# A two-layer decoder kernel: products of constants ahead of the second stage's attention, its loads issued in two parts, and the fifth stage's keys and values prepared in the third stage and kept in DRAM

## The chip, the cores and the metric

The kernel runs on one core of one Trainium2 chip. The metric is the device time of one execution in microseconds (us); lower is better. All times here are of the kernel before the change.

## What is computed

A decoder of two layers works on x of 2048 tokens (32 sequences of 64) by 256 features, all in float32. Six sub-layers follow each other, each x = x + f(layernorm(x)):

```python
x = x + attention_L0(ln(x))        # 16 heads of 128, with biases
x = x + cross_L0(ln(x), ctx, ctx)  # 32 query heads of 8, 8 key heads, no mask
x = x + ffn_L0(ln(x))              # gated, 1024 wide, gate modulated by a small attention
x = x + memory_L1(ln(x))           # cumulative sums of cos and sin features
x = x + cross_L1(ln(x), ctx, ctx)  # 16 heads of 16, rms norm of q and k, rope, causal
x = x + ffn_L1(ln(x))              # gated, 2048 wide, 4-bit weights
```

For this change two lines of the reference matter. The second sub-layer is a plain softmax attention over 64 context rows. In the fifth, keys and values come from the context alone, so they can be computed at any time:

```python
q, k = rms_norm(q, q_norm_w), rms_norm(k, k_norm_w)      # k, v: ctx, the same for all of x
q, k = q * cos + rotate_half(q) * sin, k * cos + rotate_half(k) * sin
```

## The kernel before, in words

**Tiles.** x stays in SBUF as 16 tiles (`NT`) of 128 tokens by 256 features, two sequences to a tile. Each of five stages opens with a block `token_stats` (mean and variance of every token, a square root on ACT, a reciprocal on DVE) and ends in a barrier of all engines. The fifth Python stage holds the last two sub-layers; this text calls the sub-layers "stages" one to six, as the tile names do (s2, s3a, s3f, s5a, s6f).

**Order.** Nothing schedules the work: each engine has its own program, written with `run_steps` (L87). It gets parts with a lag each; at step s the part of lag l works on unit s - l. Engines meet at counted semaphores (`wait_ge`, `then_inc`).

**Stage two** (`stage_L0_cross`, L611 to 825) has 32 units, two (r = 0 and 1) for each tile. For one unit PE does `scores` (8 products of 32x64 by 256 columns, L786), `turn(0)` and `turn(1)` (4 transposes of 128x128 each, L798), `weigh(0)` and `weigh(1)` (8 products each, L814), and once per tile `turn_x` (2 transposes, L774). DVE takes the maximum (L714) and subtracts it (L718); both read the one scores buffer, and `scores` of the next unit waits for `shifted`. ACT does the exponential (L740) and copies the turned weights out of PSUM (L746). POOL normalises x (L678) and spreads the keys (L682). PE's order within a step is scores, weigh(0), turn(0), weigh(1), turn(1), turn_x. All 8 loads of the context are issued by SP inside the `token_stats` block, two for each chunk of 4 tiles (L631, L633).

**Stage three's feed-forward** (`feed_forward`, L1190) has 32 units (4 groups of 4 tiles by 8 slices). A unit is 13 products of 512 columns (L1244, L1253) and 12 of 256 (L1264), all in the fp32r type. DVE multiplies (L1293), ACT copies the high part (L1282), POOL subtracts the low part (L1316), and `down` of the unit comes two steps later.

**Stage five** (`stage_L1_cross`, L1968) issues 5 loads beside `token_stats`, then has a block s5k in which DVE squares, norms and ropes the keys (L2018 to 2057) and POOL spreads the values (L2065, L2071), and then `attention16` (L838) in mode "L1". PE's order there is scores, turn(0), final, turn_qk, turn(1), weigh(0), turn_att, weigh(1). The 32 loads of stage six's weights are issued by SP beside it (L2191).

**Stage six** is `token_stats` with 16 BATCH_NORM_STATS (L213), then `split_tokens` and `feed_forward`.

Of the kernel before, what the change touches and what calls it, by code (L numbers as in the profile page):

```python
# [16 lines left out]
P = 128  # L17
# [106 lines left out]
class Core:  # L124


    def __init__(self, nc, ctx, ins):
# [5 lines left out]
        self.stats_ready = False  # L133
        self.stored_weights = nc.dram_tensor("stored_weights", (PIECES, P, 6 * D), F32, kind="Internal").ap()
# [475 lines left out]
def stage_L0_cross(core):  # L610
# [7 lines left out]
    with ExitStack() as octx:  # L618
# [9 lines left out]
        def load_context(sp):  # L628
            for n in range(NT // CHUNK):
# [11 lines left out]
        with ExitStack() as ctx:  # L641
# [122 lines left out]
            def _(pe):  # L764
                pe.wait_ge(zeroed, 1)

                def turn_x(u, rnd, n):
# [55 lines left out]
                run_steps(pe, U, [(scores, 3), (weigh(0), 5), (turn(0), 4), (weigh(1), 5), (turn(1), 4),  # L823
# [10 lines left out]
def attention16(core, mode, tag, mv, rstd, factor, w, zT=None, mT=None, beside=None, prefetch=None):  # L834
# [6 lines left out]
    with ExitStack() as ctx:  # L841
# [58 lines left out]
        def _(dve):  # L900
            nc.vector.tensor_copy(ident_r[:, :], core.c("ident")).then_inc(masks, 1)
            nc.vector.tensor_copy(mask_r[:, :], core.c("mask_add")).then_inc(masks, 1)
            if own:
                dve.wait_ge(zeroed, 2)

# [41 lines left out]
            steps(dve, [(attended, 4), (shift, 2)] + ([(spread_values, 1)] if own else []) + [(finish, 5)])  # L947

        @block.gpsimd
        def _(pool):  # L950
# [29 lines left out]

            steps(pool, [(residual if own else rope, 0)])
# [4 lines left out]
        def _(act):  # L986
# [56 lines left out]

            if own:
# [7 lines left out]
        def _(pe):  # L1052
            pe.wait_ge(masks, 2)

# [135 lines left out]
def feed_forward(core, tag, zT, gate_w, up_w, down_w, F, kind, mod=None, ready=None, stats=False):  # L1190
# [11 lines left out]
    with ExitStack() as ctx:  # L1202
# [10 lines left out]
        block = ctx.enter_context(nc.Block())  # L1213

# [58 lines left out]
        def _(act):  # L1273
# [5 lines left out]
            def high(u, rnd, f):  # L1279
# [4 lines left out]
            run_steps(act, U, split_modulation(True, act) + [(activate, 0), (high, 0)],  # L1284
                      unroll=FC)

        @block.vector
        def _(dve):
# [7 lines left out]
            def add(u, rnd, f):  # L1296
# [11 lines left out]
            run_steps(dve, U, split_modulation(False, dve) + [(multiply, 0), (add, 2)],  # L1308
                      unroll=FC)

        @block.gpsimd
        def _(pool):
# [6 lines left out]
            run_steps(pool, U, [(low, 0)], unroll=FC)  # L1319

def stage_L0_ffn(core):
    nc, ins = core.nc, core.ins
    F, R = 1024, 16
    with ExitStack() as ctx:
# [17 lines left out]
        w["in"] = room.sb("in", [P, NC, F])  # L1346
        w["up"] = room.sb("up", [P, NC, F])
        w["down"] = room.sb("down", [P, F // P, D])
# [122 lines left out]
        def part_of(name):  # L1471
# [5 lines left out]
                     stats=True)  # L1477
# [490 lines left out]
def stage_L1_cross(core, prefetch):  # L1968
    nc, ins = core.nc, core.ins
    H, KV, E = 16, 4, 16  # L1970
    W = KV * E
    with ExitStack() as ctx:
# [5 lines left out]
        q_cos = room.sb("q_cos", [P, D])  # L1978
        q_sin = room.sb("q_sin", [P, D])
# [3 lines left out]
        with ExitStack() as sctx:  # L1983
            sroom = Room(nc, sctx, "s5k")
            raw = sroom.sb("raw", [P, NT, W])
            values = sroom.sb("values", [P, NT, 2, W])
            qw = sroom.sb("qw", [P, D])
            kn = sroom.sb("kn", [P, NT, W])
            rot = sroom.sb("rot", [P, NT, W])
            kw = sroom.sb("kw", [P, W])  # L1990
            ss = sroom.sb("ss", [P, NT])
            root = sroom.sb("root", [P, NT])
            inv = sroom.sb("inv", [P, NT])
            loaded, step_done, rooted, summed, v_done = sroom.sems("loaded", "step_done", "rooted", "summed", "v_done")

            def load_context(sp):
                sp.dma_start(raw[:, :, :].rearrange("p t d -> p (t d)"), ins["ctx_rows"]).then_inc(loaded, 16)
                sp.dma_start(kw[:, :], ins["L1_xattn_k_norm_w"].rearrange("(a n) -> a n", a=1).to_broadcast([P, W])) \
                    .then_inc(loaded, 16)
                sp.dma_start(qw[:, :], ins["L1_xattn_q_norm_w"].rearrange("(a n) -> a n", a=1).to_broadcast([P, D])) \  # L2000
                    .then_inc(loaded, 16)
                sp.dma_start(wo[:, :, :], ins["L1_woT"].rearrange("(c p) n -> p c n", p=P)).then_inc(loaded, 16)
                sp.dma_start(values[:, :, :, :].rearrange("p t b d -> p (t b d)"), ins["ctx_values"]).then_inc(loaded, 16)
# [341 lines left out]
```

## Time and profile before

| what | value |
|---|---|
| median of 3 runs | 1947.82 us (1945.99 to 1949.38) |
| the profiled execution's own time | 1944.22 us |
| its span | 1942.4 us |
| mean granted TensorE clock | 0.902 of full speed |
| PE busy | 1711.3 us (88%) |
| DVE busy | 1134.2 us (58%) |
| ACT busy | 842.3 us (43%) |
| POOL busy | 686.1 us (35%) |

The span runs from the first to the last instruction; the time of the execution is 1.8 us longer. Busy PE time counts matmuls from start to modelled end, so a high share doesn't say at what clock the engine ran. The clock stands apart: it is granted at full speed (1.00, 2.4 GHz) or at half (0.50, 1.2 GHz). The stages, by the trace: one to 568 us, two to 761, three to 1086 (its feed-forward from 948), four to 1508, five to 1639, six to the end.

### The profile page before, as it was taken

To read this page: it belongs to the slowest core of one execution; us is meant where nothing else is said; L and a number is where in the kernel's file an instruction comes from. 1 tells how busy PE (TensorE), PEld (TensorE's weight loads), DVE (VectorE), ACT (ScalarE), POOL (GpSimd) and SP (SyncE) were. 2 spreads that over 40 slices of the span, in tenths; PEclk is the share of its full clock that TensorE was granted. 3 is DMA by queue.
4 is the path that set the end of the run, shared out by engine and by line. 5 is a ranking of instruction groups with operands and counts; after the bars stand their busy time and mean duration, and the time that the engine had idled before them with its cause. 6 is when DMAs were issued, how large, how long until landed. Compare 5 with 4: busy or idle time off the path is not lost. (4 is left out here: it accounts for less than half of the span.)

```text
span 1942.4 us, 33715 instructions
## 1 busy us (share of the span) xinstructions
PE 1711.3 (88%) x12986; PEld 1324.9 (68%) x12986; DVE 1134.2 (58%) x1820; ACT 842.3 (43%) x1399; POOL 686.1 (35%) x508
## 2 busy tenths in 40 slices
PE   4999999999959996889999786899998297999997
PEld 3888888888846665668788562444444275788886
DVE  6676767676765555565322495999897666211111
ACT  3555555555533433444422325555562275322222
POOL 0111221122123431640122204999996341223232
PEclk9999999999975555789999896999999598899999
DMA  3011111111120002000000000000000440000001
GB/s 94 15 58 55 63 38 57 54 62 38 57 98 2 1 2 92 2 2 2 2 1 1 19 18 0 1 1 1 0 1 0 157 146 2 1 1 1 1 0 43
DMA packets 49490, 57.56 MB, mean 30 GB/s; under 512 B 7216, under 2 KB 43568, under 8 KB 49248
## 3 DMA queue, kind: packets, MB, share of 16 engines
q1 hardware_dynamic: 49376, 55.97, 8.9%
q8 instruction: 80, 1.31, 0.3%
q14 instruction: 34, 0.28, 0.0%
HBM read 41.28 MB, written 14.68 MB: 29 GB/s over the span
## 5 line engine op out<-in xcount | busy, mean ns | idle before, releaser
L543 POOL TENSOR_TENSOR s_w_parts<-s_w_raw,s_w_parts 128x768 fp32r<-128x768 f32 x16 | 29.7, 1854 | 428.8 <-ACT s_w_parts L495 428.8
L1293 DVE TENSOR_TENSOR s6f_hid<-s6f_act_sb,s6f_u_ps 128x512 f32<-128x512 f32 x64 | 44.0, 687 | 219.5 <-PE s6f_u_ps L1244 219.5
L1316 POOL TENSOR_TENSOR s6f_hid_parts<-s6f_hid,s6f_hid_parts 128x512 fp32r<-128x512 f32 x64 | 82.7, 1293 | 230.5 <-ACT s6f_hid_parts L1282 230.5
L1826 POOL TENSOR_TENSOR s4b_pcs<-s4b_cs,s_p_rows 128x1024 f32<-128x1024 f32 x64 | 120.8, 1913 | 95.4 <-ACT s4b_cs L1872 95.4
L1837 POOL TENSOR_TENSOR s4b_with_re<-s4b_with_re,s4b_with_im 128x1024 f32<-128x1024 f32 x64 | 150.9, 2385 | 2.6 <-DVE s4b_with_im L1791 2.6
L1912 PE MATMUL s4b_c_ps<-s4b_pcs,const 128*128 128x512 f32 x256 | 122.3, 600 | 0.0
L419 PE MATMUL s_v_ps<-s_wv_parts,s_xnT 128*128 128x256 f32 x768 | 103.8, 285 | 12.0 <-ACT s_v L524 6.4
L478 PE MATMUL s_o_ps<-s_w_parts,s_zT 128*128 128x256 f32 x768 | 110.2, 294 | 4.1 <-DVE x_rows L582 4.1
L419 PEld LDWEIGHTS s_v_ps<-s_wv_parts,s_xnT 128*128 128x128 f32 x768 | 96.3, 191 | 17.6 <-ACT s_v L524 9.7
L1902 PE MATMUL s4b_turns_ps<-s_theta_bd,s_zc 128*128 128x512 f32 x128 | 78.1, 694 | 31.4 <-DVE s4b_frac L1776 30.4
L1316 POOL TENSOR_TENSOR s3f_hid_parts<-s3f_hid,s3f_hid_parts 128x512 fp32r<-128x512 f32 x32 | 41.3, 1291 | 180.2 <-ACT s3f_hid_parts L1282 180.2
L1264 PEld LDWEIGHTS s6f_o_ps<-s6w_parts,s6f_hid_parts 128*128 128x128 f32 x768 | 99.1, 188 | 6.6 <-issue 1.0
L1282 ACT ACTIVATE s6f_hid_parts<-s6f_hid 128x512 fp32r<-128x512 f32 x64 | 40.5, 632 | 145.1 <-PE s6f_o_ps L1264 140.9
L478 PEld LDWEIGHTS s_o_ps<-s_w_parts,s_zT 128*128 128x128 f32 x768 | 97.0, 192 | 8.8 <-issue 4.5
L1244 PE MATMUL s6f_g_ps<-s_zT,s6w_parts 128*128 128x512 f32 (+1 forms) x384 | 101.8, 401 | 1.2 <-PEq L257 1.2
L437 PE MATMUL s_q_ps<-s_xnT,s_w_parts 128*128 128x512 f32 x384 | 102.5, 403 | 0.0
L1264 PE MATMUL s6f_o_ps<-s6w_parts,s6f_hid_parts 128*128 128x256 f32 x768 | 100.5, 279 | 0.8 <-POOL s6f_hid_parts L1316 0.8
L1244 PE MATMUL s6f_u_ps<-s_zT,s6w_parts 128*128 128x512 f32 (+1 forms) x384 | 101.1, 399 | 0.0
L437 PE MATMUL s_k_ps<-s_xnT,s_w_parts 128*128 128x512 f32 x384 | 98.6, 392 | 0.0
L1912 PEld LDWEIGHTS s4b_c_ps<-s4b_pcs,const 128*128 128x128 f32 x256 | 49.4, 194 | 61.1 <-issue 58.9
L508 ACT ACTIVATE s_ex<-s_sc 128x256 f32<-128x256 f32 x64 | 26.7, 417 | 144.9 <-DVE s_sc L576 144.9
L1244 PEld LDWEIGHTS s6f_u_ps<-s_zT,s6w_parts 128*128 128x128 f32 x384 | 73.0, 190 | 17.7
(305 smaller groups left out, 4138.4 us busy)
## 6 DMA issues: line engine op xcount, KB each, us to landing
stored_weights<-s1q_halves SPq DMA_DIRECT2D x16, 768.0 KB, 3.5
s6w_parts<-stored_weights SPq DMA_DIRECT2D x32, 384.0 KB, 7.5
s1q_packed<-in_codes SPq DMA_DIRECT2D x8, 384.0 KB, 4.3
s1q_scale<-in_scale_rows SPq DMA_DIRECT2D x8, 384.0 KB, 5.0
x_rows<-in_x SPq DMA_DIRECT2D x1, 2048.0 KB, 8.2
s_w_raw<-in_L_attn_W_Q SPq DMA_DIRECT2D x16, 128.0 KB, 2.2
s_w_raw<-in_L_attn_W_K SPq DMA_DIRECT2D x16, 128.0 KB, 2.4
s_w_raw<-in_L_attn_W_O SPq DMA_DIRECT2D x16, 128.0 KB, 2.4
```

The costliest lines, as they stand in the source:

```text
L419: last = nc.tensor.matmul(v_ps[:, n * 2 * E:(n + 1) * 2 * E], xnT[:, px, c, g * TG + t, :], wv_parts[:, pw, c, :, :], start=(c == 0 and (p ...
L437: last = nc.tensor.matmul(ps[:, :], weights(slot, pw, m, c), xnT[:, px, c, g * TG:(g + 1) * TG, :], start=(c == 0 and (pw, px) == PARTS[0] ...
L478: last = nc.tensor.matmul(o_ps[:, t // 2, (t % 2) * D:(t % 2 + 1) * D], zT[:, pz, t * P:(t + 1) * P], w_parts[:, k // G, pw, 2, :], start= ...
L1244: last = nc.tensor.matmul(ps[:, s, :], wt(pw, c, f), zT[:, pz, c:c + 1, bass.ds(rnd * TG, TG), :] .rearrange("p c t q -> p (c t) q"), star ...
L1264: last = nc.tensor.matmul(o_ps[:, t, 0:D], hid_parts[:, f % 2, ph, t * P:(t + 1) * P], down_w(pw, f), start=(f == 0 and (ph, pw) == PARTS[0]),
L1282: nc.scalar.activation(hid_parts[:, f % 2, 0, :], hid[:, f % 2, :], ACT.Copy).then_inc(high_done, 1)
L1293: nc.vector.tensor_tensor(hid[:, f % 2, :], act_sb[:, f % 2, :], u_ps[:, f % 2, :], ALU.mult) \
L1316: nc.gpsimd.tensor_tensor(hid_parts[:, f % 2, 1, :], hid[:, f % 2, :], hid_parts[:, f % 2, 0, :], ALU.subtract).then_inc(low_done, 1)
L1826: last = nc.gpsimd.tensor_tensor(pcs[:, half, n_, :].rearrange("p (k c) -> p k c", k=HK), cs[:, half, n_, :].rearrange("p (k c) -> p k c", ...
L1837: nc.gpsimd.tensor_tensor(with_re[:, half, n_, :], with_re[:, half, n_, :], with_im[:, half, n_, :], op).then_inc(sum_done, 1)
L1902: nc.tensor.matmul(turns_ps[:, :], zc[:, half, bass.ds(i * P, P)], theta_bd[:, half, n_ * 64:(n_ + 1) * 64, :].rearrange("p c m -> p (c m) ...
L1912: last = nc.tensor.matmul(c_ps[:, n_, b * 512:(b + 1) * 512], core.c("tri"), pcs[:, half, n_, b * 512:(b + 1) * 512], start=True, stop=True)
```

## The change

Four parts:

1. Stage two: in its first steps PE also multiplies constants (`ident` by `age`, 128x128 by 512 columns in float32) into the buffer `o_ps`, whose content nothing reads before it is written anew. Four stand ahead of the first `turn_x`, one behind the first `scores`, one behind the second.
2. Stage two: beside `token_stats` SP issues the two loads of the first chunk alone; the other six are issued in the attention's block.
3. Stage five: keys, the tables of the queries' rope and the spread values are computed in stage three's feed-forward (class `EarlyKeys`), one instruction in a unit on DVE (units 2 to 18), one on ACT (unit 4) and two on POOL (units 4 and 8). They use the SBUF of the raw weights, whose split parts are done. SP writes them to three DRAM tensors. Stage five loads these (4 DMAs) and has no block s5k.
4. Stage five's attention also computes `shift` (ahead) and one BATCH_NORM_STATS per tile, one step behind the tile's last addition. Stage six's `token_stats` then has none.

The diff, cut to its core:

```diff
-        def load_context(sp):
-            for n in range(NT // CHUNK):
+        def load_context(sp, first=0, last=1):
+            for n in range(first, last):
...
+            @block.sync
+            def _(sp):
+                load_context(sp, 1, NT // CHUNK)
...
+                def keep_busy(first, later):
+                    def part(u, rnd, n):
+                        if not isinstance(u, int) or u > 1:
+                            return
+                        for _ in range(later if u else first):
+                            nc.tensor.matmul(o_ps[:, :], core.c("ident"), core.c("age"), start=True, stop=True)
+                    return part
...
-                run_steps(pe, U, [(scores, 3), (weigh(0), 5), (turn(0), 4), (weigh(1), 5), (turn(1), 4),
+                run_steps(pe, U, [(keep_busy(4, 0), 2), (scores, 3), (keep_busy(1, 1), 3), (weigh(0), 5), (turn(0), 4), (weigh(1), 5), (turn(1), 4),
                                   (turn_x, 2)], unroll=2, head=U + 5)
...
             if own:
                 dve.wait_ge(zeroed, 2)
+            else:
+                nc.vector.scalar_tensor_tensor(out=w["shift"][:, :], in0=mv[:, :, 0], scalar=-1.0, in1=factor[:, :],
+                                               op0=ALU.mult, op1=ALU.mult).then_inc(masks, 1)
...
+            def gather_stats(i, rnd, k):
+                dve.wait_ge(f_out, i + 1)
+                nc.vector.bn_stats(core.stats[:, i, :], core.x[:, i, :])
...
+            if not own:
+                pool.wait_ge(w["loaded"], 64)
             steps(pool, [(residual if own else rope, 0)])
...
+            if not own:
+                act.wait_ge(masks, 3)
...
             pe.wait_ge(masks, 2)
+            if not own:
+                pe.wait_ge(w["loaded"], 64)
...
-            run_steps(pool, U, [(low, 0)], unroll=FC)
+            run_steps(pool, U, [(low, 0)] + ([(early.gpsimd, 0)] if early else []), unroll=FC)
...
+class EarlyKeys:
...
+    def sync(self, sp):
...
+        sp.wait_ge(self.step_done, 16)
+        sp.dma_start(core.early_keys, self.spread).then_inc(self.stored, 16)
+        sp.dma_start(core.early_tables, self.tables).then_inc(self.stored, 16)
+        sp.wait_ge(self.v_done, 2)
+        sp.dma_start(core.early_values, self.vbd[:, :, :, :, :, :].rearrange("p t b v h e -> p (t b v h e)")) \
+            .then_inc(self.stored, 16)
+        sp.wait_ge(self.stored, 48)
...
+        elif u == 6:
+            dve.wait_ge(done, 3)
+            nc.vector.tensor_tensor(self.kn, self.raw, self.inv.unsqueeze(2).to_broadcast([P, NT, W]), ALU.mult) \
+                .then_inc(done, 1)
...
-        with ExitStack() as sctx:
-            sroom = Room(nc, sctx, "s5k")
...
+        def load_early(sp):
+            sp.dma_start(keys[:, :, :].rearrange("p t d -> p (t d)"), core.early_keys).then_inc(loaded, 16)
+            sp.dma_start(tables[:, :, :].rearrange("p a n -> p (a n)"), core.early_tables).then_inc(loaded, 16)
+            sp.dma_start(vbd[:, :, :, :, :, :].rearrange("p t b v h e -> p (t b v h e)"), core.early_values) \
+                .then_inc(loaded, 16)
+            sp.dma_start(wo[:, :, :], ins["L1_woT"].rearrange("(c p) n -> p c n", p=P)).then_inc(loaded, 16)
+
+        token_stats(core, mv, rstd, "s5n", "eps_rms5", factor, prefetch=load_early)
...
+        core.stats_ready = True
```

PE at the start of stage two, before (L774 is `turn_x`, L786 `scores`, L798 `turn`, L814 `weigh`):

```order
L763 UNCONDITIONAL_BRANCH
L774 MATMUL s_x_ps<-const,s_xn 128x128 x2
L786 MATMUL s_s_ps<-s_kbd,s_xT 64x256 x16
L798 MATMUL s_pT_ps<-const,s_ex 128x128 x8
L774 MATMUL s_x_ps<-const,s_xn 128x128 x2
L786 MATMUL s_s_ps<-s_kbd,s_xT 64x256 x8
L814 MATMUL s_o_ps<-s_vbd,s_probT 64x18 x8
```

The same place in the changed kernel (L779 is `keep_busy`; the others are L789, L801, L813, L829):

```order
L770 UNCONDITIONAL_BRANCH
L779 MATMUL s_o_ps<-const 128x512 x4
L789 MATMUL s_x_ps<-const,s_xn 128x128 x2
L801 MATMUL s_s_ps<-s_kbd,s_xT 64x256 x8
L779 MATMUL s_o_ps<-const 128x512
L801 MATMUL s_s_ps<-s_kbd,s_xT 64x256 x8
L779 MATMUL s_o_ps<-const 128x512
L813 MATMUL s_pT_ps<-const,s_ex 128x128 x8
L789 MATMUL s_x_ps<-const,s_xn 128x128 x2
L801 MATMUL s_s_ps<-s_kbd,s_xT 64x256 x8
L829 MATMUL s_o_ps<-s_vbd,s_probT 64x18 x8
```

Six products are new, all ahead of the third unit's scores; from there on the order is as it was.

DVE in the changed kernel, in stage three's feed-forward, units 3 to 9 (L1327 is the multiplication of a unit, L1334 and L1339 end a group of tiles, L1424 to 1439 are of `EarlyKeys`):

```order
L1327 TENSOR_TENSOR s3f_hid<-s3f_act_sb,s3f_u_ps 128x512
L1424 TENSOR_REDUCE s_tables<-s_kn 128x16
L1262 TENSOR_TENSOR s_m_rows<-s_mT,s_m_rows 16x512
L1327 TENSOR_TENSOR s3f_hid<-s3f_act_sb,s3f_u_ps 128x512 x2
L1427 RECIPROCAL s_tables<-s_tables 128x16
L1262 TENSOR_TENSOR s_m_rows<-s_mT,s_m_rows 16x512
L1327 TENSOR_TENSOR s3f_hid<-s3f_act_sb,s3f_u_ps 128x512
L1430 TENSOR_TENSOR s_kn<-s_all,s_tables 128x1024
L1327 TENSOR_TENSOR s3f_hid<-s3f_act_sb,s3f_u_ps 128x512
L1434 TENSOR_TENSOR s_kn<-s_kn,s_tables 128x1024
```

Each of the moved instructions stands behind a unit's multiplication, ahead of the next one's. SP in the changed kernel, at the start of stage five:

```order
L2153 DMA s_keys<-early_keys 128x4096
L2154 DMA s_tables<-early_tables 128x512
L2155 DMA s_vbd<-early_values 128x4352
L2157 DMA s_wo<-in_L_woT 128x2x256
L189 UNCONDITIONAL_BRANCH
L910 UNCONDITIONAL_BRANCH
L2278 DMA s6w_parts<-stored_weights 128x3x256 x32
```

These four stand where five stood, ahead of stage six's 32 weight loads as before; they bring 4.6 MB.

## Rows read from the trace of the kernel before

**Rows 1.** The page: busy tenths and granted clock in 40 slices of 48.6 us
```profile
PE   4999999999959996889999786899998297999997
PEclk9999999999975555789999896999999598899999
```

**Rows 2.** Windows: us, PE, PEld, DVE, ACT, POOL busy, clock, DMA share, GB/s
```profile
577.60:760.40 182.80, 171.80 (x1822) 123.03 (x1822) 95.91 (x128) 72.73 (x112) 69.57 (x78) 0.50 0.02 6
641.73:652.98 11.25, 10.78 (x114) 7.71 (x115) 6.00 (x8) 4.52 (x8) 4.54 (x6) 0.50 0.01 1
1598.10:1625.80 27.70, 26.42 (x446) 21.45 (x430) 17.29 (x25) 19.00 (x38) 9.13 (x16) 1.00 0.01 2
```

**Rows 3.** Timeline of stage two at half clock, PE in the unit with turn_x
```profile
646.87 1.16 PE L786 MATMUL s_s_ps<-s_kbd,s_xT 32*64 32x256 f32 x16
...
648.94 1.12 PE L798 MATMUL s_pT_ps<-const,s_ex 128*128 128x128 f32 x4
649.98 1.05 PE L814 MATMUL s_o_ps<-s_vbd,s_probT 128*64 128x18 f32 x16
...
652.98 1.16 PE L786 MATMUL s_s_ps<-s_kbd,s_xT 32*64 32x256 f32 x16 [0.47 <-ACT s_xT L757]
```

**Rows 4.** Timeline of stage five at full clock: the same kinds of work
```profile
1603.12 0.69 PE L1113 MATMUL s5a_s_ps<-s5a_kbd,s5a_qT 32*64 32x128 f32 x32
1603.74 0.66 PE L1125 MATMUL s5a_pT_ps<-const,s5a_ex 128*128 128x128 f32 x4
1603.92 1.22 DVE L919 TENSOR_REDUCE s5a_mx<-s5a_s_ps 128x16 f32<-128x1024 f32 x1 [0.64 <-PE s5a_s_ps L1113]
1605.18 1.22 DVE L923 TENSOR_TENSOR s5a_sc<-s5a_s_ps,s5a_mx 128x1024 f32<-128x1024 f32 x1
```

**Rows 5.** Groups by line in stage two: count, busy, mean ns, idle before
```profile
L746 ACT ACTIVATE s_probT<-s_pT_ps 128x512 f32<-128x512 f32 x64 | 38.2, 596 | 32.3 <-PE s_pT_ps L798 32.3
L740 ACT ACTIVATE s_ex<-s_sc 128x1024 f32<-128x1024 f32 x32 | 33.8, 1057 | 3.3 <-DVE s_sc L718 3.3
```

**Rows 6.** Windows where the clock stood half or full, columns as in rows 2
```profile
550.40:555.00 4.60, 0.66 (x4) 0.42 (x4) 3.97 (x8) 1.59 (x3) 0.00 (x0) 1.00 0.00 0
1484.00:1508.00 24.00, 16.73 (x86) 10.97 (x82) 11.00 (x12) 4.86 (x11) 6.83 (x6) 1.00 0.00 0
1541.00:1551.80 10.80, 8.23 (x88) 6.37 (x88) 4.90 (x4) 6.45 (x14) 5.24 (x9) 0.50 1.09 349
1647.00:1657.50 10.50, 9.94 (x32) 5.07 (x32) 9.71 (x30) 5.88 (x16) 0.00 (x0) 0.50 0.01 2
```

**Rows 7.** Timelines: stage two's first work; a float32 product of 512 columns at half clock
```profile
574.38 1.23 POOL L678 TENSOR_SCALAR s_xn<-x_rows,s_mv,s_rstd 128x256 f32<-128x256 f32 x1 [5.75 <-SPq L641]
...
1220.44 1.80 PE L1902 MATMUL s4b_turns_ps<-s_theta_bd,s_zc 128*128 128x512 f32 x2 [1.89 <-DVE s4b_frac L1776]
```

**Rows 8.** Timeline of stage five's start
```profile
1508.44 0.35 SPq L1997 DMA_DIRECT2D s5k_raw<-in_ctx_rows  x1
...
1518.44 8.05 POOL L2065 TENSOR_TENSOR s_vbd<-s5k_values,const 128x4096 f32<-128x4096 f32 x1 [21.59 <-DMA s5k_values<-in_ctx_values]
...
1521.54 6.04 DVE L2024 TENSOR_TENSOR s5k_kn<-s5k_raw,s5k_inv 128x1024 f32<-128x1024 f32 x1
...
1537.02 0.72 POOL L972 TENSOR_TENSOR s5a_q_rows<-s5a_yt,s_q_cos 128x256 f32<-128x256 f32 x1 [8.95 <-ACT s5a_yt L989]
...
1539.50 0.66 PE L1093 MATMUL s5a_qk_ps<-const,s5a_q_rows 128*128 128x128 f32 x2 [32.27 <-POOL s5a_q_rows L978]
```

**Rows 9.** DMA issues of the page: count, KB each, us from issue to landing
```profile
x_rows<-in_x SPq DMA_DIRECT2D x1, 2048.0 KB, 8.2
```

**Rows 10.** Timeline: stage three's feed-forward, a unit's POOL work and the products that read it
```profile
965.44 1.29 POOL L1316 TENSOR_TENSOR s3f_hid_parts<-s3f_hid,s3f_hid_parts 128x512 fp32r<-128x512 f32 x1 [3.18 <-ACT s3f_hid_parts L1282]
...
971.93 1.58 PE L1264 MATMUL s3f_o_ps<-s_down_parts,s3f_hid_parts 128*128 128x256 f32 x12
```

**Rows 11.** Timeline of stage six's start
```profile
1638.90 5.32 DVE L213 BATCH_NORM_STATS2 x_stats<-x_rows 128x6 f32<-128x256 f32 x16 [0.32 <-PEq L841]
```

More of the change, by code:

```diff
@@ L945, in finish @@
                     nc.vector.tensor_tensor(core.x[:, i, :], core.x[:, i, :], f_rows, ALU.add).then_inc(f_out, 1)
-            steps(dve, [(attended, 4), (shift, 2)] + ([(spread_values, 1)] if own else []) + [(finish, 5)])
+            def gather_stats(i, rnd, k):
+                dve.wait_ge(f_out, i + 1)
+                nc.vector.bn_stats(core.stats[:, i, :], core.x[:, i, :])
+            steps(dve, [(attended, 4), (shift, 2)] + ([(spread_values, 1)] if own else []) + [(finish, 5)] +
+                  ([] if own else [(gather_stats, 6)]))
         @block.gpsimd
@@ L1213, in feed_forward, with _ @@
         block = ctx.enter_context(nc.Block())
+        if early:
+            @block.sync
+            def _(sp):
+                early.sync(sp)
         def split_modulation(engine_is_scalar, eng):
@@ L1282, in high @@
                 nc.scalar.activation(hid_parts[:, f % 2, 0, :], hid[:, f % 2, :], ACT.Copy).then_inc(high_done, 1)
-            run_steps(act, U, split_modulation(True, act) + [(activate, 0), (high, 0)],
-                      unroll=FC)
+            run_steps(act, U, split_modulation(True, act) + [(activate, 0), (high, 0)] +
+                      ([(early.scalar, 0)] if early else []), unroll=FC)
         @block.vector
@@ L1306, in add @@
                                            core.x[:, bass.ds(rnd * TG + j, 1), :].rearrange("p t n -> p (t n)"))
-            run_steps(dve, U, split_modulation(False, dve) + [(multiply, 0), (add, 2)],
-                      unroll=FC)
+            run_steps(dve, U, split_modulation(False, dve) + [(multiply, 0), (add, 2)] +
+                      ([(early.vector, 0)] if early else []), unroll=FC, head=3 * FC if early else None)
         @block.gpsimd
@@ L1345, in stage_L0_ffn @@
         m_rows = room.sb("m_rows", [64 + R, NT, P], F32R)
-        w["in"] = room.sb("in", [P, NC, F])
-        w["up"] = room.sb("up", [P, NC, F])
-        w["down"] = room.sb("down", [P, F // P, D])
+        w["all"] = room.sb("all", [P, 3, NC * F])
+        for n, (name, c) in enumerate((("in", NC), ("up", NC), ("down", F // P))):
+            w[name] = w["all"][:, n, :].rearrange("p (c n) -> p c n", c=c)
         high_done, low_done, zeroed = room.sems("high_done", "low_done", "zeroed")
@@ L2075, in stage_L1_cross @@
-        attention16(core, "L1", "s5a", mv, rstd, factor, {"q_cos": q_cos[:, :], "q_sin": q_sin[:, :], "shift": shift, "keys": keys, "wo": wo, "values": vbd},
-                    prefetch=prefetch)
+        (loaded,) = room.sems("loaded")
+        def load_early(sp):
[4 more added lines that the diff above has]
+            sp.dma_start(wo[:, :, :], ins["L1_woT"].rearrange("(c p) n -> p c n", p=P)).then_inc(loaded, 16)
@@ L2082 @@
+        token_stats(core, mv, rstd, "s5n", "eps_rms5", factor, prefetch=load_early)
+        attention16(core, "L1", "s5a", mv, rstd, factor,
+                    {"q_cos": tables[:, 0, :], "q_sin": tables[:, 1, :], "shift": shift, "keys": keys, "wo": wo,
+                     "values": vbd, "loaded": loaded}, prefetch=prefetch)
+        core.stats_ready = True
 PIECES = 16
```

201 lines of the change are left out of this document (115 added, 86 removed).

## The prediction

> **What bounds the kernel now.** I read the page first, its line of slices, for the clock. PE is busy nearly everywhere, yet in slices 12 to 15, which lie in stage two, the granted clock is 5 tenths [rows 1]. Then windows: all of stage two's attention, 182.8 us, ran at 0.50, the level of 1.2 GHz, with PE busy in 171.8 of them [rows 2]. A tile (two units) takes 11.25 us there: PE 10.78, DVE 6.00, POOL 4.54, ACT 4.52 [rows 2]. So PE bounds this stage, and it does so because it runs at half speed. The timeline shows the same inside a unit: scores to the next scores takes 6.11 us with turn_x, a transposition takes 1.04 us, and the one gap (0.47 us) is the copy xT behind turn_x [rows 3]; the tile's other unit is left with 11.25 - 6.11 = 5.14 us, all of it PE.
>
> How fast the same work is at full clock, stage five tells, which ran at 1.00 in its later part and took 27.7 us for five tiles, 5.54 each, PE busy 26.4 [rows 2]. Its scores hand over after 0.62 us (1603.12 to 1603.74), and their reduction starts 0.80 us after their start [rows 4].
>
> Why does stage two run at half clock? The clock had been full to 555 us with PE busy in only 0.66 of the last 4.6 us, and after that gap the stage starts low [rows 1, 6]. It doesn't come back by itself, though PE is busy 95% of the time. Stage five, by contrast, began at 0.50 too (PE busy 8.2 of 10.8 us) and stands at 1.00 later [rows 2, 6], and before it the clock was held at 1.00 over 24 us with PE busy in only 16.7 [rows 6]. Stage two's own mix of short products doesn't raise the clock; something else has to. The change puts six products of 512 columns in its fill, back to back in part, where PE was idle.
>
> **The sum, part by part.** The profiled execution took 1944.2 us, 3.6 below the median of 1947.8; the sum is made against the former and 3.6 is added at the end. A measurement can tell about 0.2%, 4 us, from no change.
>
> *Stage two, the clock.* I forecast that the clock rises in the fill and stays up. Then PE's share of a tile halves to 5.4 us and another loop bounds it: scores and their reduction share one buffer. From scores' start to the reduction 0.80, reduction 1.22, hand-over 0.04, subtraction 1.22 [rows 4], and some 0.14 to the next scores: 3.42 us a unit, 6.8 a tile. That is the lower bound. ACT has 1.06 for the exponential and 0.60 for each of two copies in the same unit [rows 5], and xT in every second; they queue in order, and the unit with xT has to wait for that copy, as now. Following the queues with these lengths I get 3.45 and 4.05 us, 7.5 a tile. The upper bound is 8.6: both units lose a further half microsecond to queueing. 16 tiles by 11.25 - 7.5 = 3.75 give **-60** (-71 to -42). What is left of fill and drain, 182.8 - 180 us, gives another 2 back.
>
> *Stage two, the products.* A float32 product of 512 columns takes 1.80 us at half clock [rows 7]. Four stand ahead of the first turn_x and delay it by at most 7.2 us; the two others take 1 to 3.6 us, mostly while PE would wait for the first reductions. Against this, SP has six issues fewer ahead of the block, and POOL, which began at 574.38, had been waiting for SP since 568.6 [rows 7]; I give that 3 us. POOL also has to build xn and the spread keys first, about 3 us. Net **+1** (-2 to +4).
>
> *Stage three's feed-forward.* It receives 15 DVE instructions of mostly about 1.2 us (as L923 of the same size [rows 4]), some 17 us, one ACT root with its table load, and on POOL the spreading of values, 8.05 us [rows 8], plus 1.6 us. PE bounds this stage. Each DVE instruction stands behind its unit's multiplication, and what it delays is the next multiplication, which is needed later than it comes; I cost them at nothing. POOL is the doubtful place: `low` ended at 966.73 and its reader started at 971.93 [rows 10], slack 5.2, and 8.05 us exceed that by some 2.9 minus what the queue of that engine stands idle anyway. And there is sharing: L2024 took 6.04 us where its like take 1.2, and it ended just after L2065 did, at 1526.5 [rows 8]. The same could hold a multiplication up in unit 5 or 6. I take **+0.5** (0 to +3). The Trainium skill (SBUF — State Buffer, on the port pair that VectorE and GpSimd share) describes such a lock; by it alone, with DVE shut out for all of POOL's 8 us, the cost would be the +3 of this range, and the row above agrees with it. SP's stores wait for values and keys on their own queue, with nothing behind them but the end of the block: nothing. Were every moved instruction to delay PE by its length, it would be 17 + 10 = +27.
>
> *Stage five's start.* Now 31.1 us pass from the first load's issue (1508.44) to PE's first product (1539.50) [rows 8]: loads, POOL's 8 us, DVE's chain, then rope. After: four loads (4.6 MB), then rope from 1537.02 to 1539.50, 2.5 us [rows 8]. 2 MB landed in 8.2 us, 256 GB/s with its latency [rows 9]; the window with the weight loads moved 349 GB/s [rows 6]. 4.6 MB take 13.2 to 18 us; I take 14.5, plus 2.5 is 17: **-14** (-10 to -17). The statistics of the tokens, square root and shift are done well within it. If this cover went, DVE's single shift would be next. In the steady part gather_stats adds 0.4 us a tile to DVE, busy 17.3 of 27.7 us and waiting [rows 2]: nothing.
>
> *Stage six's start.* 16 statistics of 5.32 us go [rows 11]; the last tile's own, one step behind, costs 0.45: **-4.9** (-3.5 to -5.3).
>
> Sum: -60 - 2 + 1 + 0.5 - 14 - 4.9 = -79.4, so 1864.8 for a profiled execution and **1868** for the median.
>
> **Rivals.** *The clock rises but does not hold, or does not rise.* For it: this mix at half clock never raised it in 180 us at 94% PE busy [rows 2], and stage six's transposes stayed at 0.50 with PE busy 9.9 of 10.5 us [rows 6], so transposes count for little, and they are two fifths of a unit's PE time. Against: at full clock the same work is done in two thirds of the time, so it is denser, and the 24 us held at 1.00 with PE 70% busy show that it can be held with PE less busy than this [rows 6]. Its price: -62 becomes 0, and +1 becomes +2, the sum -16: 1931. Chance 0.11. The Trainium skill (TensorE: Matmul & The Clock Gate, Part 4: PE-mode transpose) says that transpose mode doesn't count as PE busy in the same way; by it stage two would fall back soon after the six products, and the time would be this rival's. That the transposing window stayed low agrees with it.
> *The clock holds for a part of stage two* and falls at some hiccup: each tile lost costs 3.75; a quarter to all but one lost gives 1884 to 1929. Chance 0.07.
> *Slower.* Stage five rises to full clock now after a slow first 12 us; its start is changed, with no pause for PE to fill and other waits between the first tiles. If the clock rose neither there nor in stage two, a tile of stage five would take 5.54 by 1.5, the ratio 11.25 to 7.5 of stage two's tile, 8.3 us, and 15 tiles give +42: 1931 + 42 = 1973. It decides from a loss of +17 on, 6 tiles. Against: nothing in the tile's work has changed and the rise came in its first tiles. Chance 0.02.
> *No effect:* the clock stays low in stage two (-16 in all, above), and the moved instructions delay the feed-forward by half of their 27 us: 1945, which can't be told from before. Chance 0.02.
> The rest, 0.78, is the forecast, with 1857 to 1886 from the bounds of stage two's tile.
>
> **How the numbers follow.** The time is the forecast's, 1868. Its bounds leave out 0.22; the range reaches down to 1856 and up to 1912, into the case of a part held, so that about 0.18 is left out. Every case but the last two is faster by far more than 4 us: faster 0.96, same 0.02, slower 0.02.
>
> **What would show it.** In the changed profile the clock of slices 12 to 15 reads 9, DVE's reduction and subtraction follow each other with little idle time, and a tile of stage two takes 7.5 us; PE is no longer the engine that ends the waits there. Half clock in those slices with a tile of 11.25 means that the first rival holds. Stage three's unit keeps its length, apart from a dent in units 4 to 6. From the first load of stage five to PE's first product 17 us pass; 25 would mean that the loads are slower than I took them. At the start of stage six no group of 16 statistics is left. What would make the forecast wrong in size is the loop of stage two: a tile of 8.6 us adds 18 us.

## The result, and the profile after

The changed kernel takes 1866.3 us (median of 4 runs, 1862.4 to 1867.5), the kernel before 1948.6 beside it (1946.0 to 1949.4): a ratio of 0.9576, 95% interval 0.9558 to 0.9595. The prediction was 1868. One thing has to be known to read the numbers below: the kernel before has a second time of its own, 1881 to 1891 us, which it took in 5 of the 26 runs beside the experiments; what it is, the experiments show, the ratio above is against its usual time, and against the second time the changed kernel's gain is only 1% (1865.7 beside three such runs at 1881.4, 1884.8 and 1891.3).

The profiled execution has a span of 1860.6 us, 81.8 less. Between the square roots on ACT at the start of each stage (`s2n_std` and its like, one per stage in both traces; below they are called the roots; read to 0.1 us) the time went so:

| stretch | before | after | difference |
|---|---|---|---|
| root of stage two to root of stage three | 198.0 | 133.5 | -64.5 |
| three to four | 330.1 | 329.3 | -0.8 |
| four to five | 417.3 | 419.1 | +1.8 |
| five to six (all of stage five, six's statistics) | 130.5 | 113.6 | -16.9 |
| six to the end | 296.9 | 295.8 | -1.1 |

The page's slices are 46.5 us now:

```profile
PE   4999999999987886799999777999998598999997
PEclk9999999999998996899999778999999797999999
```

Against [rows 1] the four slices of 5 tenths are gone; PE is busy a smaller share of stage two, at twice the clock. The windows of the attention, of one tile of it, and of five tiles of stage five (columns as in [rows 2]):

```profile
576.60:694.40 117.80, 102.83 (x1826) 74.07 (x1826) 92.58 (x126) 72.29 (x112) 67.78 (x76) 1.00 0.03 9
640.55:647.68 7.13, 6.32 (x114) 4.60 (x115) 5.81 (x9) 4.44 (x8) 4.54 (x5) 1.00 0.01 2
1520.00:1547.70 27.70, 26.44 (x432) 21.46 (x430) 19.02 (x31) 19.55 (x40) 9.14 (x16) 1.00 0.01 3
```

A tile takes 7.13 us instead of 11.25, and stage five's five tiles take the same 27.7 us with 1.7 us more DVE work in them (the statistics). Who bounds a tile of stage two now, its timeline says (start, length, engine, line, idle time before and its releaser):

```profile
640.55 0.69 PE L801 MATMUL s_s_ps<-s_kbd,s_xT 32*64 32x256 f32 x16 [0.47 <-ACT s_xT L764]
...
641.34 1.23 DVE L721 TENSOR_REDUCE s_mx<-s_s_ps 128x16 f32<-128x1024 f32 x1 [0.75 <-PE s_s_ps L801]
...
642.60 1.22 DVE L725 TENSOR_TENSOR s_sc<-s_s_ps,s_mx 128x1024 f32<-128x1024 f32 x1
...
643.97 0.69 PE L801 MATMUL s_s_ps<-s_kbd,s_xT 32*64 32x256 f32 x16 [0.17 <-DVE s_sc L725]
...
646.83 0.38 PE L789 MATMUL s_x_ps<-const,s_xn 128*128 128x128 f32 x2
...
647.24 0.38 ACT L764 ACTIVATE s_xT<-s_x_ps 128x256 f32<-128x256 f32 x1 [1.84 <-PE s_x_ps L789]
...
647.68 0.69 PE L801 MATMUL s_s_ps<-s_kbd,s_xT 32*64 32x256 f32 x16 [0.47 <-ACT s_xT L764]
```

The first unit lasts 3.42 us and is the loop of scores, reduction and subtraction: PE's next scores wait for DVE's subtraction. In the second, 3.71 us, PE works without a gap from scores to turn_x, and the next scores wait for the copy xT. PE's fill (the products are L779):

```profile
570.24 5.71 PE L779 MATMUL s_o_ps<-const 128*128 128x512 f32 x8 [5.56 <-PEq L189]
...
575.78 0.38 PE L789 MATMUL s_x_ps<-const,s_xn 128*128 128x128 f32 x2
...
576.63 0.69 PE L801 MATMUL s_s_ps<-s_kbd,s_xT 32*64 32x256 f32 x16 [0.47 <-ACT s_xT L764]
...
577.25 1.13 PE L779 MATMUL s_o_ps<-const 128*128 128x512 f32 x2
...
580.06 0.69 PE L801 MATMUL s_s_ps<-s_kbd,s_xT 32*64 32x256 f32 x16 [1.68 <-DVE s_sc L725]
```

The clock went to 1.00 at 574.3, within the first four (5.71 us for the 8 records of 4 products, two to a product: the first ones follow each other after 0.85, the last after 0.43), and stayed there until 697.2, after the stage's end. Stage five's start:

```profile
1444.55 0.34 SPq L2153 DMA_DIRECT2D s_keys<-early_keys  x1
...
1459.31 0.72 POOL L995 TENSOR_TENSOR s5a_q_rows<-s5a_yt,s_tables 128x256 f32<-128x256 f32 x1 [26.36 <-DMA s_wo<-in_L_woT]
...
1461.79 0.66 PE L1122 MATMUL s5a_qk_ps<-const,s5a_q_rows 128*128 128x128 f32 x2 [18.46 <-POOL s5a_q_rows L1001]
```

17.2 us from the first load to PE's first product, where it was 31.1 [rows 8]. And where the price was looked for, in stage three's feed-forward:

```profile
906.07 7.02 POOL L1481 TENSOR_TENSOR s_vbd<-s_all,const 128x4096 f32<-128x4096 f32 x1
...
908.38 0.69 DVE L1327 TENSOR_TENSOR s3f_hid<-s3f_act_sb,s3f_u_ps 128x512 f32<-128x512 f32 x1 [5.03 <-ACT s3f_act_sb L1311]
...
910.94 2.69 DVE L1262 TENSOR_TENSOR s_m_rows<-s_mT,s_m_rows 16x512 fp32r<-16x512 f32 x1 [1.71 <-ACT s_m_rows L1259]
...
913.05 1.75 POOL L1350 TENSOR_TENSOR s3f_hid_parts<-s3f_hid,s3f_hid_parts 128x512 fp32r<-128x512 f32 x1
...
915.73 1.56 PE L1298 MATMUL s3f_o_ps<-s_down_parts,s3f_hid_parts 128*128 128x256 f32 x12
```

While POOL spreads the values (7.02 us), the multiplication, which has an operand in PSUM, takes its usual 0.69 us; L1262, with both in SBUF, takes 2.69 instead of 0.70 and ends just after POOL does. The next multiplication stands behind L1262 in DVE's order and is held up with it: ACT had its operand ready at 911.53, PE the other at 911.47, and it starts at 913.66:

```profile
910.93 0.60 ACT L1311 ACTIVATE s3f_act_sb<-s3f_g_ps 128x512 f32<-128x512 f32 x1
913.66 0.69 DVE L1327 TENSOR_TENSOR s3f_hid<-s3f_act_sb,s3f_u_ps 128x512 f32<-128x512 f32 x1
```

`low` is 3 us late too. Their reader `down` isn't: PE shows no wait here.

### The profile page after: what moved, and what is told of

It reads as the page before. It is cut to its first block and busy times, and to the rows that moved or that the text cites. A ratio compares the mean times of both kernels' runs of the same rounds, so it can differ in the third digit from the quotient of the medians.

```text
span 1860.6 us, 33694 instructions
## 1 busy us (share of the span) xinstructions
PE 1647.9 (89%) x12998; PEld 1277.9 (69%) x12998; DVE 1129.8 (61%) x1820; ACT 843.3 (45%) x1401; POOL 684.4 (37%) x508
## 5 line engine op out<-in xcount | busy, mean ns | idle before, releaser
L1327 DVE TENSOR_TENSOR s6f_hid<-s6f_act_sb,s6f_u_ps 128x512 f32<-128x512 f32 x64 | 44.0, 688 | 218.3 <-PE s6f_u_ps L1278 218.3
L1278 PE MATMUL s6f_u_ps<-s_zT,s6w_parts 128*128 128x512 f32 (+1 forms) x384 | 100.4, 396 | 0.0
```

Source lines behind the costliest of these rows:

```text
L1278: last = nc.tensor.matmul(ps[:, s, :], wt(pw, c, f), zT[:, pz, c:c + 1, bass.ds(rnd * TG, TG), :] .rearrange("p c t q -> p (c t) q"), star ...
L1327: nc.vector.tensor_tensor(hid[:, f % 2, :], act_sb[:, f % 2, :], u_ps[:, f % 2, :], ALU.mult) \
```

## The experiments

Theory 1: the products raise the clock in stage two's fill, it then holds, and the rest of the change adds up beside it. Theory 2: something else raises it, or is needed for it (the split loads, the earlier start). The later experiments ask which products do it, and whether they have to be products.

**The products alone**, in the kernel before (with `keep_busy` as in the change):

```diff
-                run_steps(pe, U, [(scores, 3), (weigh(0), 5), (turn(0), 4), (weigh(1), 5), (turn(1), 4),
+                run_steps(pe, U, [(keep_busy(4, 0), 2), (scores, 3), (keep_busy(1, 1), 3), (weigh(0), 5), (turn(0), 4), (weigh(1), 5), (turn(1), 4),
```

> The kernel before with the six products alone. If the products are what raises the clock (theory 1), stage two runs at 1.00 with a tile of 7.1 us, as in the changed kernel, and the time is 1948 - 63 = 1885 us (in the changed kernel stage two takes 64.5 us less; 1 to 2 of them may belong to the split loads). If the shorter issuing of loads is needed for it, since PE then starts sooner after its last work (theory 2), the clock stays at 0.50 and the time is 1948 to 1955.

Measured: 1890.1 us (four runs: 1893.9, 1886.4, 1885.7, 1894.0), the kernel before beside it at 1943 to 1950 in five runs and at 1884 in two. Theory 1 stands: no split is needed. Against the two runs at 1884, though, it gains nothing: what the products give is the time that the kernel before now and then has without them. The median is 5 us less gain than expected; two of the four runs (1885.7 and 1886.4) are where 1885 was expected, and what parts them from the two at 1894, of which one was profiled, is open. In that trace the first products start at 574.96 and the first scores at 581.69, 11.3 us after the stage's root; in the changed kernel that is 7.3, in the kernel before 8.0. The products cost 3.3 us where the other six loads are still issued ahead of them, and the clock rose later (579.7).

**The change without the products**:

```diff
-                run_steps(pe, U, [(keep_busy(4, 0), 2), (scores, 3), (keep_busy(1, 1), 3), (weigh(0), 5), (turn(0), 4), (weigh(1), 5), (turn(1), 4),
+                run_steps(pe, U, [(scores, 3), (weigh(0), 5), (turn(0), 4), (weigh(1), 5), (turn(1), 4),
```

> The changed kernel without the six products; all else stays. Theory 1: stage two goes back to 0.50 and 11.25 us a tile, 1866 + 63 to 65 = 1930 us, which is also the sum of the other parts, 1948 - 14 - 4.7 = 1929. Theory 2: the clock rises without them and the time stays near 1866.

Measured: 1926.6 us (1923.2 to 1928.2, four runs); stage two at 0.50 throughout. Theory 1: the products are worth 60 us (from 1926.6 to 1866.3), the rest 20.5 (from 1947.1 to 1926.6). First scores come 5.1 us after the root instead of 8.0: the split loads alone give 2.9, which with 13.8 for stage five's start and 4 for stage six's makes 20.7.

**Transpositions in place of the products**:

```diff
-                            nc.tensor.matmul(o_ps[:, :], core.c("ident"), core.c("age"), start=True, stop=True)
+                            for _ in range(7):
+                                nc.tensor.transpose(o_ps[:, 0:P], core.c("ident"), core.c("ident"))
```

> The changed kernel with each product of 512 columns replaced by seven transpositions of 128x128 (7 x 0.26 us at half clock is a product's 1.80): 28 ahead of the first turn_x, 7 and 7 later. If any work of PE of this length raises the clock, the time is 1866 as with products. If transpositions count for less than products do (stage six's 10 us of them stayed at 0.50), stage two stays at 0.50: 1930 us.

Measured: 1867.5 us (1862.7 to 1868.0, four runs). PE, and the window of the attention:

```profile
571.78 5.81 PE L780 MATMUL s_o_ps<-const 128*128 128x128 f32 x28 [5.56 <-PEq L189]
...
578.90 0.98 PE L780 MATMUL s_o_ps<-const 128*128 128x128 f32 x7
```

```profile
577.50:696.40 118.90, 102.76 (x1839) 74.93 (x1837) 92.92 (x128) 72.76 (x113) 67.71 (x76) 1.00 0.04 12
```

The clock rose at 577.05, within them, and held. So transpositions, back to back, do here what products do. But those of stage six at 0.50 [rows 6] remain, and they differ in more than their place. In stage two one transposition follows the other after 0.21 us; in stage six, in the kernel before, 32 of them took 10.5 us:

```profile
1648.80 8.55 PE L302 MATMUL s6t_turned<-const,s6t_xn 128*128 128x128 f32 x26 [0.40 <-DVE s6t_xn L277]
```

That is one in 0.33 us; they come in pairs, one pair every 0.65 us, and read data where those of stage two read a constant. In none of the thirteen traces did the clock rise while those of stage six ran, nor while the like ones of stages three and four did. The prediction's "PE busy 9.9 of 10.5 us" counts each from its start to its modelled end, which lies 0.42 to 0.49 us later, so it does not show that PE had no room. Whether the spacing or the data makes the difference no run tested.

**The statistics alone**, in the kernel before (`gather_stats` and `stats_ready` as in the change):

> The kernel before with the gathered statistics of stage five alone. By the two traces PE's first transposition of stage six follows the last addition of stage five by 4.0 us instead of 8.7: 1948 - 4.7 = 1943 us. Rival: one instruction of 0.41 us more per tile on DVE delays the additions that PE waits for, and stage five grows by up to 16 x 0.1 = 1.7 us (its attention took 100.3 us instead of 98.7 in the changed kernel): 1945 us.

Measured: 1942.8 and 1943.9 us in two runs, 1875.9, 1881.2 and 1885.6 in three. The two belong beside the kernel before at 1943 to 1950 (median 1947.1): 3.8 less. The three belong beside its two runs at 1884.2: 3.0 less by the median. The profiled one, at half clock in stage two, shows the end of stage five:

```profile
1641.31 0.42 DVE L945 TENSOR_TENSOR x_rows<-x_rows,s5a_va_ps 128x256 f32<-128x256 f32 x1 [1.86 <-PE s5a_va_ps L1180]
1641.65 0.74 DVE L949 BATCH_NORM_STATS2 x_stats<-x_rows 128x6 f32<-128x256 f32 x2
...
1645.34 0.91 PE L302 MATMUL s6t_turned<-const,s6t_xn 128*128 128x128 f32 x3 [4.07 <-DVE s6t_xn L277]
```

4.0 us from the last addition to the first transposition, as in the changed kernel; before it was 8.7. Its attention takes 98.4 us from PE's first product to the last addition, the kernel before 98.7: the rival's 1.7 us isn't there. The three others are the surprise: the gathered statistics lie 900 us behind stage two and can't raise its clock. The kernel before beside it does the same in two of seven runs. Which executions have it is luck as far as the runs show: nothing in the kernel decides it. The burst in mid-stage, below, caught one such rise in a profile.

**The first four products alone**:

```diff
-                run_steps(pe, U, [(keep_busy(4, 0), 2), (scores, 3), (keep_busy(1, 1), 3), (weigh(0), 5), (turn(0), 4), (weigh(1), 5), (turn(1), 4),
+                run_steps(pe, U, [(keep_busy(4, 0), 2), (scores, 3), (weigh(0), 5), (turn(0), 4), (weigh(1), 5), (turn(1), 4),
```

> The changed kernel with the four products ahead of the first turn_x alone. In the changed kernel the clock rose at 574.3 us, while these four ran. If raising it is all that is needed, every run takes 1866 us. If the two later products are needed to hold it over the sparse steps of the fill (PE idle 2 us before the second scores), some or all runs fall back to 0.50 and take 1930.

Measured: 1929.3 us (1925.5 to 1930.1), none of four at 1866. Windows before and after its clock falls, and PE's timeline between:

```profile
573.60:580.30 6.70, 3.49 (x39) 1.39 (x38) 2.45 (x2) 2.21 (x3) 5.98 (x5) 1.00 0.90 283
580.30:763.00 182.70, 169.81 (x1804) 122.27 (x1790) 97.26 (x138) 72.95 (x112) 64.89 (x74) 0.50 0.02 6
```

```profile
576.44 0.69 PE L801 MATMUL s_s_ps<-s_kbd,s_xT 32*64 32x256 f32 x16 [0.47 <-ACT s_xT L764]
579.87 0.78 PE L801 MATMUL s_s_ps<-s_kbd,s_xT 32*64 32x256 f32 x16 [2.73 <-DVE s_sc L725]
```

The four raise the clock to 1.00 at 573.5, and it is lost at 580.3, after a stretch with PE idle for 2.7 us between the first scores. It is not regained in the 180 us behind. Four runs can't tell, here or in the change without the products, whether the rise by luck of the kernel before (5 in 26) has become rarer; they do tell that the four products don't make it certain.

**The two later products alone**:

```diff
-                run_steps(pe, U, [(keep_busy(4, 0), 2), (scores, 3), (keep_busy(1, 1), 3), (weigh(0), 5), (turn(0), 4), (weigh(1), 5), (turn(1), 4),
+                run_steps(pe, U, [(scores, 3), (keep_busy(1, 1), 3), (weigh(0), 5), (turn(0), 4), (weigh(1), 5), (turn(1), 4),
```

> The changed kernel with the two later products alone. Without the four first ones PE has 1.8 us of extra work at half clock behind each of the first two scores. If the rise needs a stretch without gaps, these two seldom give it: 1930 us in most runs, 1866 in some, as the kernel before has it now and then by luck (2 of 7 runs at 1884). If any added work at the fill is enough: 1866 in all.

Measured: 1870.0 us (1863.3 to 1871.5), all four runs near the changed kernel's time. Windows before and after the rise:

```profile
576.70:586.00 9.30, 8.47 (x46) 3.90 (x46) 4.90 (x4) 1.10 (x2) 6.62 (x5) 0.50 0.54 180
586.00:698.00 112.00, 98.24 (x1780) 71.80 (x1780) 88.28 (x124) 69.90 (x110) 62.54 (x72) 1.00 0.01 2
```

My expectation was the wrong way round in both: the two products in the gaps between the first scores, 3.6 us of PE work in all by the 1.80 us of [rows 7], do by themselves what the six do, for 4 us more (the clock rose at 586.1, 9 us after the first scores; in the changed kernel it rose before them); the four in front alone do nothing that lasts.

**A burst in the middle of the stage**, in the kernel before:

```diff
+                def burst(u, rnd, n):
+                    if not isinstance(u, int) or u != 12:
+                        return
+                    for _ in range(12):
+                        nc.tensor.matmul(x_ps[:, 256:512], core.c("ident"), core.c("age")[:, 0:256], start=True, stop=True)
...
-                run_steps(pe, U, [(scores, 3), (weigh(0), 5), (turn(0), 4), (weigh(1), 5), (turn(1), 4),
+                run_steps(pe, U, [(scores, 3), (burst, 3), (weigh(0), 5), (turn(0), 4), (weigh(1), 5), (turn(1), 4),
```

> The kernel before with 12 products of 256 columns behind the scores of unit 12 of stage two, nothing at its start. Theory: what keeps the clock at 0.50 is only that nothing raises it, and once up it holds on this mix wherever it was raised. Then the first 6 tiles take 11.25 us, the last ten 7.1, the burst costs 5 to 11 us: 1948 - 10 x 4.1 + 8 = 1915 (1910 to 1920). Rival: only a burst in front of the stage, with PE's queues empty, raises it: 1948 + 11 = 1959.

Measured: 1915.3 and 1914.6 us in two runs (mean clock 0.926), 1891.8 and 1891.3 in the others (0.945). The first pair is the forecast to a microsecond, and the kernel before has no time between 1891 and 1943 us in 30 runs. So the clock was very likely raised in mid-stage and held from there; that is argued from times and mean clocks, since neither run of the pair was profiled. The profiled run is of the second pair, and shows the luck itself. Its windows, and the burst, which comes at 623.9 us:

```profile
571.00:587.40 16.40, 5.30 (x44) 3.01 (x44) 5.27 (x7) 3.46 (x6) 9.83 (x7) 0.50 0.60 192
587.40:706.00 118.60, 103.46 (x1804) 76.20 (x1804) 89.11 (x127) 70.47 (x111) 63.06 (x73) 1.00 0.01 2
```

```profile
L771 PE MATMUL s_x_ps<-const x24: 379/379/483, 623.9 to 629.0; 128*128 128x256 f32 x24
```

The clock rose at 587.4, before the burst, on instructions that are the kernel before's own; in the profile of the kernel before these same instructions left it at 0.50.

**Products at the other cold stretches**, on the changed kernel, in `token_stats` and in `attention16`:

```diff
+        bursts = {'s3n': 14, 's4n': 4, 's5n': 18}.get(tag, 0)
...
+            @block.tensor
+            def _(pe):
+                for _ in range(bursts):
+                    nc.tensor.matmul(busy_ps[:, :], core.c("ident"), core.c("age"), start=True, stop=True)
...
+            if not own:
+                for _ in range(14):
+                    nc.tensor.matmul(qk_ps[:, :], core.c("ident"), core.c("age"), start=True, stop=True)
             pe.wait_ge(masks, 2)
```

> The changed kernel with such products also where PE idles ahead of other cold stretches: 14 in the statistics block of stage three, 4 in stage four's, 18 in stage five's, and 14 in stage five's attention while it waits for its loads. In the changed kernel the clock is 0.50 for 31 us at stage three's start, 20 and 24 us in stage four, 27 us at stage five's. If they stay at 1.00, what PE bounds there shrinks: stage five's first 13.7 us by some 5, stage three's products of the weights by 4, others 1 to 3: 1855 us. Rival: split_tokens is bound by DVE as much as by PE, the clock falls within it again, and bursts that begin at half clock run past the block: 1866 to 1872.

Measured: 1875.3 us (1873.0 to 1883.9), slower than the changed kernel with a higher mean clock (0.963, the changed kernel 0.952). Most of it is an error of size: I took a product for 0.43 us; it is two records, 0.87. Stage five's stretch:

```profile
1449.24 15.69 PE L209 MATMUL s5n_busy_ps<-const 128*128 128x512 f32 x36 [1.26 <-PEq L168]
1465.22 12.25 PE L1091 MATMUL s5a_qk_ps<-const 128*128 128x512 f32 x28 [0.30 <-PEq L189]
1477.32 0.38 PE L1134 MATMUL s5a_qk_ps<-const,s5a_q_rows 128*128 128x128 f32 x2
```

The bursts outlast the waits they were to fill, 28.1 us instead of 17.2. Behind them stage five's attention takes 95.7 us instead of 100.3: there the clock is worth 4.6. From root to root stage five is 6.2 us longer (119.8). In stage three nothing is won (331.7 us from root to root, 329.3 without the burst). The clock, at 1.00 from 700.7, falls to 0.50 at 714.3, 2.2 us after the transpositions of `split_tokens` begin, and stays there while they run: 24 of them took 7.9 us, spaced as in stage six. In stage four it falls 1.2 us after they begin. So transpositions spaced like that did not hold a clock that was up, which is what the first rival feared for stage two.

**Bursts of the right size, in stage five alone**, and the changed kernel beside them. The first edit is against the kernel with all bursts:

```diff
-        bursts = {'s3n': 14, 's4n': 4, 's5n': 18}.get(tag, 0)
-                for _ in range(14):
+        bursts = {'s5n': 9}.get(tag, 0)
+                for _ in range(9):
```

> The changed kernel with 9 products in stage five's statistics block and 9 in its attention while PE waits for the loads. With 18 and 14 (f2_all_bursts) stage five ran at 1.00 from its first product on and its attention took 95.7 us instead of 100.3, but at 0.86 us each the products ran past both waits (PE's first real work 28.1 us after the first load, not 17.2). 9 x 0.86 = 7.7 us fits each wait (8.7 and 8.5 us). If the clock then holds likewise: 4 to 5 us less than g_after_again, 1862 to 1863. Rival: the gaps that are left let the clock fall as before, the time is that of g_after_again.

The second edit, against that one (the burst's block in `token_stats` goes too):

```diff
-        bursts = {'s5n': 9}.get(tag, 0)
```

> As f3_s5_bursts with the 9 products of the attention's wait alone; they start at 0.50 (1.7 to 1.8 us each) or late at 1.00. If the clock rises 4 us after they begin, as in stage two, five take half clock and the rest full, 5 x 1.75 + 4 x 0.86 = 12 us against a wait of 8.5: 3.5 us late, 4.6 gained, 1865 to 1866. If it rises later, slower than g_after_again by up to 7 us.

> The changed kernel once more, on the chip of f3 and f4: 1866 us (1862 to 1868). If the clock of stage two rose there by luck too, a run in some of these would be at 1930; theory 1 with the two later products says none.

Measured, six runs each: 1861.2 us with both bursts (1859.9 to 1865.6), 1863.0 with the second alone (1861.5 to 1865.0), 1865.7 for the changed kernel (1862.7 to 1867.3). With both:

```profile
1451.22 7.96 PE L209 MATMUL s5n_busy_ps<-const 128*128 128x512 f32 x18 [1.27 <-PEq L168]
1459.95 7.96 PE L1091 MATMUL s5a_qk_ps<-const 128*128 128x512 f32 x18 [0.77 <-PEq L189]
1468.48 0.41 PE L1134 MATMUL s5a_qk_ps<-const,s5a_q_rows 128*128 128x128 f32 x2 [0.56 <-POOL s5a_q_rows L1010]
```

Both fit (17.3 us from the first load), and the attention takes 96.6. With the second burst alone the clock rises 5.0 us after the burst's start, PE's first work comes 1.9 us late (19.1) and the attention takes 95.8. With both, the median is 4.5 us, 0.24%, below the changed kernel, with ranges that overlap: it is the lowest of the kernels measured, by as much as can just be told. The changed kernel was near 1866 in all six runs, the kernel before beside it at 1881 to 1891 in three of twelve and at 1947 to 1953 in nine.

## Why the prediction was right, and where it was not

| step | predicted | measured |
|---|---|---|
| stage two, tiles, fill and drain | -62 | -65.0 (182.8 to 117.8) |
| stage two, products and split loads | +1 | -0.7 (8.0 to 7.3 us from root to scores) |
| stage three | +0.5 | -0.8, no wait on PE |
| stage four | 0 | +1.8 |
| stage five's start | -14 | -13.8 |
| stage five's attention | 0 | +1.7 |
| stage six's start | -4.9 | -4.7 |
| the span in all | -79.4 | -81.8 |

*The clock.* The outcome was right: it rose and held. Its reason was half right. "Stage two's own mix of short products doesn't raise the clock; something else has to" is the step that failed: the kernel's own instructions raise it in 5 of 26 runs, and the trace of one such rise is above. What the change does is to make certain what was luck: all 10 runs of the changed kernel took 1862 to 1868 us, and so did the four with transpositions; of all 38 runs of kernels with work in both gaps, with or without the rest, none shows the time of a stage two at half clock. And it is not the six products as such, "back to back in part", but the two that stand where PE was idle between the first scores; the four in front raise a clock that is lost again without the other two. That the same mix holds the clock at full speed over 110 us is in every trace where it rose and lasted; that at half speed it doesn't raise it in 180 us is in four traces (the kernel before, the change without products, the first four alone, the statistics alone). Where it rises by luck it does so at the start: in the trace above at 587.4, 9.5 us after PE's first work of the stage. What decides it there is open. The total has some luck of its own: 3 us more gain in the tiles and 3 us in two terms beside it stand against 3.5 us lost in stage four and stage five's attention, both forecast at 0.

*The tile.* 7.13 us, not 7.5. The unit without xT was right (3.45, measured 3.42). The unit with it I had at 4.05, it took 3.71: I let the copy xT queue behind ACT's exponential; in the trace it stands ahead of it, and behind turn_x only. Sixteen times the 0.37 between 7.5 and 7.13 is 6 us more gain, of which 3 were lost in fill and drain.

*Products and split loads.* The 3 us given to the split were right (5.1 against 8.0 us). The products I charged with 4; in the changed kernel they cost 7.3 - 5.1 = 2.2, since the clock rose while they ran.

*Early keys.* Costed at +0.5, they cost nothing that can be seen: PE's waits over 135 us of the feed-forward add up to 2.7 us in both traces. DVE got 16 instructions and 13.4 us, where the prediction counted 15 and 17. POOL's spreading was the doubtful place and delayed `low` as foreseen, by 3 us; the slack of [rows 10] covered it. A multiplication was held up too, by 2.1 us, but behind L1262 and not by a lock of its own, and the same slack covered that: the bound of +3 didn't come. The Trainium skill (SBUF — State Buffer, section "SBUF: two separate sides") limits the lock beside a POOL instruction to DVE instructions with two inputs in SBUF, or in a mode with two ports; the rows above agree: 0.69 us with an operand in PSUM, 2.69 instead of 0.70 with both in SBUF.

*Stage five's start.* 14.5 us for the loads and 2.5 for the rope were forecast, 14.8 and 2.5 measured. The volume was read too low: 128 rows of 4096, 512, 4352 and 512 floats are 4.85 million bytes, where 4.6 MB was divided by GB/s; with it the bounds are 13.9 to 19 us, and the loads came near the lower one, at 329 GB/s.

*Stage five's attention* is 1.7 us longer. It isn't the statistics, which took nothing where they were alone. The clock was at 0.50 from 1554.0 to 1557.4 in the changed kernel, in its last tiles, and stood at 1.00 there before; the products alone and the change without them have the same dip and 100.5 and 100.4 us, the statistics alone have neither. The products alone leave stage five as it was, so its own changes aren't needed for the dip. What sets it off is open. So are the 1.8 us of stage four: from root to root it took 417.3 us in the profile of the kernel before and 419.0 to 421.9 in all twelve others, of which only the one with all bursts changes anything there (420.1). So 417.3 may be the odd one; the one profile can't tell.

*The first rival* had the mechanism right that would cost the gain, and its price nearly: the first four products alone, where the clock rose and did not hold, gave 1929.3 against its 1931, the change without products 1926.6. The second rival's upper end is a slip: 15 tiles at 3.75 give 1924, not 1929. The Trainium skill (TensorE: Matmul & The Clock Gate, Part 4: PE-mode transpose) says that transpose mode doesn't count as PE busy in the same way, and stood behind it. That isn't borne out in stage two: 28, 7 and 7 transpositions raised and held the clock as products did (1867.5 us). The spaced ones of stage six, and those of stages three and four in the kernel with all bursts, behaved as it says.

## What to carry to other kernels

Where a stretch that is bound by PE runs at half clock, look at what precedes it: a few microseconds of work for PE that costs little (2 us here), in the gaps of the fill rather than ahead of it, gave 60 us here against the kernel's usual time and nothing against its lucky one, and once up, the clock held to the stage's end. Size such work by its cold and warm length, both, and let it end with the wait that it fills; a burst that outlasts it costs its length in full, whatever the mean clock says. Run a kernel often enough to see whether it has two times: this one was 3% faster by luck in one run of five, and a change that has nothing to do with it can be credited with that.

## What the runs showed of the hardware that I had not expected

- One and the same program has its clock raised in a sparse fill in some executions and not in others (5 of 26 at 1881 to 1891 us, the others at 1943 to 1956).
- Transpositions back to back, one in 0.21 us, raised the clock like products: 5.8 us of them, the clock at 1.00 from within them. Transpositions in pairs every 0.65 us did not raise it in 10.5 us in any of thirteen traces, and in two stages of one trace a clock at 1.00 fell 1.2 and 2.2 us after they began.
- At half clock stage two's mix, PE busy 171.8 of 182.8 us, did not raise it past the fill, in four traces; the same instructions with PE busy 102.8 of 117.8 us held it at 1.00.
- A DVE instruction of two inputs in SBUF took 2.69 us in place of 0.70 beside a POOL one of 7.02; one with an operand in PSUM ran in its 0.69 beside the same.
